# Expert blocks of a fused attention and mixture-of-experts kernel: first layer transposed, its weight fetched per block, GpSimd's gathers and scatters unrolled

## The chip, the cores and the metric

The kernel runs on one core of one Trainium2 chip. The metric is device time in microseconds, the median of several executions. "PE" is the matmul engine (its weight loads are listed as PEld), "DVE" the vector engine, "ACT" the scalar engine, "POOL" GpSimd, "SP" the sync engine, which here only issues DMAs.

## The reference, cut to what matters

A block of spatial attention, one of Nystrom attention, and then a mixture of experts, all in fp32, over T = 4096 tokens of D = 256 features. The change touches only the experts (E = 16, hidden size H = 512, two experts per token):

```python
def _L1_ffn_ref(x, W_gate, W1, W2):
    K = 2
    ...
    xf = x.reshape(-1, D)
    probs = jax.nn.softmax(xf @ W_gate, axis=-1)
    top_g, top_i = jax.lax.top_k(probs, K)
    gates = jnp.zeros((T, E), dtype=x.dtype).at[jnp.arange(T)[:, None], top_i].set(top_g)

    def step(y, params):
        W1e, W2e, ge = params
        h = jax.nn.gelu(xf @ W1e, approximate=False)
        return (y + ge[:, None] * (h @ W2e), None)
    y0 = jnp.zeros((T, D), dtype=x.dtype)
    y, _ = jax.lax.scan(step, y0, (W1, W2, gates.T))
    return y.reshape(B, L, D)
```

The output is the token rows before the experts plus y.

## The kernel before, in words

Each engine has a program of its own, written out by hand; semaphores alone order them against each other. Four samples pass through the two attention parts first (some 727 us). Each sample's rows go to the output in DRAM, and normalised to `rows_scratch` in DRAM. Then the tokens are sorted: DVE works out for each of 79 blocks of 128 slots (`BLOCKS` = 2T/128 + E - 1) which token stands in each slot (`token_of`), which row of the output it is added to (`row_of`; an empty slot has a number out of range, which the scatter skips), and which expert the block belongs to (`expert_of`). All slots of a block have the same expert. Meanwhile SP brings all weights of all experts into SBUF, 512 KB of `w1` and 512 KB of `w2` per expert, two experts at a time (lines 488 to 498), and the gates into `rows_scratch`.

The expert stage then runs over the 79 blocks, four to a pass of a loop (`ROUNDS` = 19 passes and three blocks behind them). For block n:

- POOL copies the block's column of `token_of` into `gather_ix` (L396), waits for that copy, and gathers 128 rows of 258 floats (256 features and two gates) from DRAM into one of four buffers `xg` (L399). This is done three blocks ahead: `add_rows` of block n first issues the gather of block n + 3.
- PE turns the rows by two transposes into a PSUM bank (`turn_rows`, through the helper line L506), DVE picks the gate (L1426, L1428) and copies the turned rows into `xgT` (L1429).
- PE multiplies them with the expert's `w1` (`hidden`, L885): the turned rows are the stationary operand, 512 columns of `w1` the moving one, for two halves of the contraction. An fp32 matmul takes two passes on PE, so this is 4 weight loads and 4 matmuls in the trace. The result has tokens on the partitions.
- ACT applies gelu into `hb` (L1046), PE transposes it by four (L506 again), DVE copies that to `hT` (L1436).
- PE multiplies `hT` with the expert's `w2` (L910, 8 matmuls of 256 columns in the trace). DVE multiplies with the gate into one of four buffers `y_sb` (L1444).
- POOL copies the block's column of `row_of` into `scatter_ix` (L406), waits for it, for `y_sb`, and for the scatter of the block before to have landed, and issues a scatter that adds the rows to the output in DRAM (L415). Two scatters may add to the same row, so they go one after the other.

PE's order in a block n is: transposes of gelu's result of n, `hidden` of n + 1, `turn_rows` of n + 2, second layer of n. The expert's number is read from SBUF into a register on PE (L889) twice per block, once for each layer. PE, ACT, DVE and POOL all run loops with register counters, except that POOL and DVE have the first four blocks written out.

```python
if u >= 1:
    pool.wait_ge(y_stored[u - 1], (i + 1) * 16)
elif again:
    pool.wait_ge(y_stored[3], i * 16)
```

These are the lines that hold a scatter back until the one before has landed; `y_stored[u]` counts 16 for each landed scatter out of buffer u.

## Time and profile before

| what | value |
|---|---|
| runs, device time | 1201.26, 1198.99, 1202.12 us |
| median | 1201.26 us |
| profiled execution: span from its first to its last instruction | 1197.8 us |
| profiled execution: time of its own | not given by the page; the runs above lie 1.2 to 4.3 us over its span |
| PE busy in the span | 1022.2 us, 85% |
| DVE, ACT, POOL busy | 690.5, 373.5, 361.4 us |
| DMA | 50.84 MB, mean 42 GB/s |

The span is the hardware profiler's record of one execution; busy time adds up an engine's instructions without its register, branch, semaphore and DMA-issuing ones (but POOL's indirect DMAs are in it). The expert stage begins with the routing at 727 us and its blocks fill the time from about 776 us to the end.

### The profile page before, as it was taken

The numbers are of one execution on the slowest core, as the hardware profiler recorded it, in microseconds if no ns is written. First come the engines' busy times: TensorE is split into PE (matmuls) and PEld (weight loads), VectorE is DVE, ScalarE is ACT, GpSimd is POOL, SyncE is SP. The second block draws the span as 40 slices with busy tenths as digits, with TensorE's granted clock in tenths as the row PEclk, the third lists the DMA queues.
The fourth block names the chain that finished last, engine by engine and source line by source line (L and its number), as shares of the span: only waits on it lengthen the run. The fifth ranks groups of instructions, "written<-read, shape, count | busy, mean of one in ns | idle before, by whom it ended". The sixth has DMA issues, their size and how long they took to land.

```text
span 1197.8 us, 20466 instructions
## 1 busy us (share of the span) xinstructions
PE 1022.2 (85%) x6163; PEld 654.5 (55%) x6164; DVE 690.5 (58%) x1665; ACT 373.5 (31%) x947; POOL 361.4 (30%) x514
## 2 busy tenths in 40 slices
PE   4999997999996999998999992378888888888886
PEld 2656654557663557664567660245555555545554
DVE  5767676766575767576776579923333333333332
ACT  3523463532464423455333551301111111111110
POOL 2220011310011400011500020545655556655654
PEclk8899998999997999997999996589999999999999
DMA  4000003000003000002000008933333333223220
GB/s 122 2 1 1 1 2 108 1 1 1 1 1 107 1 1 1 1 1 73 1 1 1 1 2 231 359 79 49 50 52 50 49 50 51 46 42 52 48 42 14
DMA packets 41262, 50.84 MB, mean 42 GB/s; under 512 B 10624, under 2 KB 32512, under 8 KB 41184
## 3 DMA queue, kind: packets, MB, share of 16 engines
q0 software_dynamic: 17344, 27.24, 11.9%
q1 hardware_dynamic: 23840, 22.56, 6.2%
q8 instruction: 48, 0.79, 0.3%
q14 instruction: 30, 0.25, 0.1%
HBM read 32.96 MB, written 18.78 MB: 43 GB/s over the span
## 4 chain that ended last, share of the span: by engine, by line
PE 53%; issue 15%; DVE 14%; DMA 8%; POOL 5%; ACT 3%; POOLq 1%; DVEq 0%; ACTq 0%
PE PS L506 10%; PE PS L574 10%; DMA low<-rows_scratch,gather_ix 7%; PE PS L758 6%; PE PS L535 6%; PE PS L910 5%; POOL out_dram L415 4%; PE PS L885 3%; PE PS L666 2%; PE PS L647 2%; DVE neg_max L1093 2%; PE PS L652 1%; PE PS L626 1%; PE PS L721 1%; DVE low L1444 1%
## 5 line engine op out<-in xcount | busy, mean ns | idle before, releaser
L361 POOL TENSOR_SCALAR aggr<-aggr 128x1 f32<-128x1 f32 x64 | 14.6, 228 | 592.7 <-DVE aggr L1155 592.7
L910 PE MATMUL PS<-arena,low 128*128 x632 | 156.8, 391 | 31.9 <-issue 30.9
L415 POOL DMA_INDIRECT out_dram<-low,scatter_ix x79 | 127.6, 1615 | 110.2 <-DVE low L1444 48.3
L506 PE MATMUL PS<-ident,arena 128*128 128x128 f32 x1024 | 144.6, 287 | 15.7 <-ACT arena L978 9.1
L1046 ACT ACTIVATE low<-PS 128x512 f32<-128x512 f32 x78 | 46.6, 597 | 350.3 <-PE PS L885 350.3
L885 PE MATMUL PS<-arena,low 128*128 x316 | 150.6, 599 | 0.4 <-issue 0.4
L506 PEld LDWEIGHTS PS<-ident,arena 128*128 128x128 f32 x1024 | 121.9, 150 | 47.8 <-issue 37.4
L910 PEld LDWEIGHTS PS<-arena,low 128*128 128x128 f32 x632 | 113.6, 189 | 61.9 <-issue 49.7
L1093 DVE TENSOR_REDUCE neg_max<-PS 128x1 f32<-128x1024 f32 (+1 forms) x97 | 118.4, 1221 | 48.6 <-PE PS L574 46.5
L574 PE MATMUL PS<-arena 128*128 128x512 f32 x256 | 126.7, 597 | 0.0
L964 ACT ACTIVATE arena<-PS,neg_max 128x1024 f32<-128x1024 f32 x64 | 71.3, 1114 | 132.4 <-DVE neg_max L1093 132.4
L969 ACT ACTIVATE arena<-PS,neg_max 128x128 f32<-128x128 f32 x256 | 89.8, 376 | 60.0 <-DVE neg_max L1093 60.0
L1444 DVE TENSOR_SCALAR low<-PS,slot_gate 128x256 f32<-128x256 f32 x79 | 38.2, 484 | 119.4 <-PE PS L910 85.4
L506 PEld LDWEIGHTS PS<-ident,low 128*128 128x128 f32 x474 | 56.7, 141 | 90.3 <-DMA low<-rows_scratch,gather_ix 77.1
L506 PE MATMUL PS<-ident,low 128*128 128x128 f32 x474 | 81.5, 281 | 24.5 <-DMA low<-rows_scratch,gather_ix 23.5
L399 POOL DMA_INDIRECT low<-rows_scratch,gather_ix x79 | 80.1, 1013 | 67.7 <-POOL gather_ix L396 63.9
L1426 DVE TENSOR_TENSOR gate_parts<-low,pick_of 128x2 f32<-128x2 f32 x79 | 12.7, 161 | 138.1 <-PE PS L506 136.1
L978 ACT COPY arena<-PS 128x1024 f32<-128x1024 f32 x64 | 64.5, 1008 | 61.0 <-PE PS L506 61.0
L535 PE MATMUL PS<-arena,low 128*128 128x512 f32 (+1 forms) x168 | 78.1, 609 | 5.1 <-DVE arena L1081 4.2
L758 PE MATMUL PS<-arena 128*128 128x256 f32 x320 | 80.9, 386 | 0.0
L885 PEld LDWEIGHTS PS<-arena,low 128*128 128x128 f32 x316 | 54.4, 192 | 39.1 <-issue 39.1
L758 PEld LDWEIGHTS PS<-arena 128*128 128x128 f32 x320 | 59.1, 190 | 28.3 <-issue 22.1
(195 smaller groups left out, 1488.8 us busy)
## 6 DMA issues: line engine op xcount, KB each, us to landing
arena<-in_L_ffn_W_dram SPq DMA_DIRECT2D x32, 512.0 KB, 5.2
arena<-in_x_dram SPq DMA_DIRECT2D x4, 1024.0 KB, 8.3
rows_scratch<-arena POOLq DMA_DIRECT2D x4, 1024.0 KB, 6.4
out_dram<-t POOLq DMA_DIRECT2D x4, 1024.0 KB, 9.1
low<-rows_scratch,gather_ix POOLq DMA_INDIRECT x79, 2.8
out_dram<-low,scatter_ix POOLq DMA_INDIRECT x79
arena<-in_L_attn_w_qkv_dram SPq DMA_DIRECT2D x1, 768.0 KB, 5.0
arena<-in_L_attn_w_out_dram SPq DMA_DIRECT2D x1, 256.0 KB, 5.5
```

What stands on the lines that cost most here:

```text
L399: pool.indirect_dma_start(xg[:, b, :], None, rows_dram, bass.IndirectOffsetOnAxis(ap=gather_ix[:, b:b + 1], axis=0)).then_inc(xg_loaded[b] ...
L415: pool.indirect_dma_start(out_rows, bass.IndirectOffsetOnAxis(ap=scatter_ix[:, u:u + 1], axis=0), y_sb[:, u, :], None, bounds_check=T - 1, ...
L506: mm = pe.transpose(PS[0:s.shape[1], dst_bank, n * P:n * P + s.shape[0]], s, ident[0:s.shape[0], 0:s.shape[0]])
L535: mm = pe.matmul(PS[0:m, bank, :], w[c], src[:, c, half * 512:half * 512 + 512], start=c == 0, stop=c == KC - 1)
L574: mm = pe.matmul(PS[:, b + k, :], ops[0], ops[1], start=True, stop=True)
L758: mm = pe.matmul(bank[:, o:o + 2 * M], RX[:, g, h, 0, :], RX[:, g, h].rearrange("p r m -> p (r m)"), start=True, stop=True)
L885: mm = pe.matmul(PS[:, 2 + p, :], xgT[:, p, c, :], w1_sb[:, bass.ds(e * (KC * H) + c * H, H)], start=c == 0, stop=c == KC - 1)
L910: mm = pe.matmul(PS[:, 6 + p, 0:D], hT[:, p, c, :], w2_sb[:, bass.ds(e * (HC * D) + c * D, D)], start=c == 0, stop=c == HC - 1)
L964: act.activation(Pm[:, u % 2, :], src, ACT.Exp, bias=neg_max[:, u % 2, 0:1], accum_out=row_sum[:, u % NT:u % NT + 1]).then_inc(s_exp, 1)
L969: ins = act.activation(Pm[:, u % 2, o:o + M], src[:, o:o + M], ACT.Exp, bias=neg_max[:, u % 2, h:h + 1], accum_out=head_sum[:, u % 2, h:h ...
L978: act.copy(PT[:, u % 2, :], PS[:, 2:4, :].rearrange("p b n -> p (b n)")).then_inc(t_act, 1)
L1093: dve.tensor_reduce(dst, src, AX.X, ALU.max, negate=True).then_inc(s_max, 1)
```

## The change

What it does:

- The first layer is made transposed. `w1` becomes the stationary operand (eight 128 x 128 pieces, 16 weight loads and 16 matmuls in the trace) and the turned rows `xgT` the moving one (128 columns), so that the hidden units stand on the partitions. Gelu writes `hT` directly. PE's four transposes of gelu's result, DVE's copy of them and `hb` go.
- `w1` is no longer held for all experts. SP brings the block's expert's 512 KB from HBM into one of four buffers `w1_now`, with an address from a register that it loads from `expert_of`; a fetch waits until the first layer of the block four before is done (`h_mm`). The 79 fetches are 41 MB where 8 MB were loaded before. `w2` stays resident and is loaded alone ahead.
- POOL's program is written out for all 79 blocks. Gather and scatter take their index column straight from `token_of` and `row_of`; the two copies, and the waits for them, go.
- PE reads the expert's number once a block instead of twice. DVE picks the gate beside the copy of the turned rows, in another order. ACT now also waits until the second layer of two blocks before has read `hT`. The first four blocks are written out on PE and ACT too.

The diff, cut to its core:

```diff
-        w1_sb = arena[:, 0:E * KC * H]
+        W1_BUFS = 4
+        w1_now = arena[:, 0:W1_BUFS * KC * H].rearrange("p (b n) -> p b n", b=W1_BUFS)
         w2_sb = arena[:, E * KC * H:E * (KC * H + HC * D)]
...
+            def gather(n):
+
+                pool.indirect_dma_start(xg[:, n % 4, :], None, rows_dram,
+                                        bass.IndirectOffsetOnAxis(ap=token_of[:, n:n + 1], axis=0)).then_inc(xg_loaded[n % 4], 16)
+
+            def add_rows(n):
+                if n + 3 < BLOCKS:
+                    pool.wait_ge(xt_mm, n + 1)
+                    gather(n + 3)
+                pool.wait_ge(y_copied, n + 3)
+
+                if n >= 1:
+                    pool.wait_ge(y_stored[(n - 1) % 4], ((n - 1) // 4 + 1) * 16)
+                pool.indirect_dma_start(out_rows, bass.IndirectOffsetOnAxis(ap=row_of[:, n:n + 1], axis=0),
+                                        y_sb[:, n % 4, :], None, bounds_check=T - 1, oob_is_err=False,
+                                        compute_op=ALU.add).then_inc(y_stored[n % 4], 16)
...
-                loaded = expert_dma[e % len(expert_dma)]
-                sp.dma_start(w1_sb.rearrange("p (e c h) -> p e c h", e=E, c=KC)[:, e],
-                             w1.rearrange("e (c p) h -> p e c h", p=P)[:, e]).then_inc(loaded, 16)
                 sp.dma_start(w2_sb.rearrange("p (e c d) -> p e c d", e=E, c=HC)[:, e],
-                             w2.rearrange("e (c p) d -> p e c d", p=P)[:, e]).then_inc(loaded, 16)
+                             w2.rearrange("e (c p) d -> p e c d", p=P)[:, e]).then_inc(expert_dma[e % len(expert_dma)], 16)
...
+            sp.wait_ge(tables_ready, 1)
+
+            def fetch_w1(n, u, again):
+
+                e = sp.value_load(expert_of[0:1, bass.ds(n, 1)], min_val=0, max_val=E - 1)
+                if again:
+                    sp.wait_ge(h_mm, n - 3)
+                sp.dma_start(w1_now[:, u, :].rearrange("p (c h) -> p c h", c=KC),
+                             w1.rearrange("e (c p) h -> e p c h", p=P)[bass.ds(e, 1)].rearrange("o p c h -> p (o c) h")).then_inc(w1_landed[u], 16)
...
-                for c in range(KC):
-                    mm = pe.matmul(PS[:, 2 + p, :], xgT[:, p, c, :], w1_sb[:, bass.ds(e * (KC * H) + c * H, H)],
-                                   start=c == 0, stop=c == KC - 1)
-                mm.then_inc(h_mm, 1)
...
+                pe.wait_ge(w1_landed[u], 16 * (r + 1))
+                if again:
+                    pe.wait_ge(gelu_done, n - 1)
+                for hc in range(HC):
+                    for c in range(KC):
+                        mm = pe.matmul(PS[:, 2 + p, hc * P:(hc + 1) * P], w1_now[:, u, c * H + hc * P:c * H + (hc + 1) * P],
+                                       xgT[:, p, c, :], start=c == 0, stop=c == KC - 1)
+                mm.then_inc(h_mm, 1)
...
-                transposes(pe, 4 + p, [hb[:, p, c * P:(c + 1) * P] for c in range(HC)]).then_inc(ht_mm, 1)
...
+                if ahead(i, u, 1):
+                    hidden(n + 1, i + (u + 1) // 4, (u + 1) % 4, again or u >= 1)
+                if ahead(i, u, 2):
+                    turn_rows((u + 2) % 4, i + (u + 2) // 4, p)
+                rows_out(n, p, expert(n))
...
+                act.wait_ge(h_mm, n + 1)
+                if again or u >= 2:
+                    act.wait_ge(y_mm, n - 1)
+                apart(act, "act")
+                act.activation(hT[:, p].rearrange("p c n -> p (c n)"), PS[:, 2 + p, :], ACT.Gelu).then_inc(gelu_done, 1)
...
-                dve.wait_ge(ht_mm, n + 2)
-                dve.tensor_copy(hT[:, p].rearrange("p c n -> p (c n)"), PS[:, 4 + p, :]).then_inc(hT_ready, 1)
```

How the change moves instructions on POOL, which issues every gather and scatter, in the first blocks of the expert stage: gather and scatter of one block before (a name in brackets is a semaphore that the instruction waits for; `gix` and `six` are those of the two copies),

```order
L396 COPY gather_ix<-token_of 128x1 [waits xt_mm]
L399 DMA low<-rows_scratch,gather_ix 128x258 [waits gix]
L406 COPY scatter_ix<-row_of 128x1
L415 DMA out_dram<-low,scatter_ix 4096x256 [waits y_stored0,six,y_copied]
L396 COPY gather_ix<-token_of 128x1 [waits xt_mm]
```

and in the changed kernel, where L392 is the gather and L403 the scatter:

```order
L392 DMA low<-rows_scratch,token_of 128x258 [waits xt_mm]
L403 DMA out_dram<-low,row_of 4096x256 [waits y_stored0,y_copied]
L392 DMA low<-rows_scratch,token_of 128x258 [waits xt_mm]
L403 DMA out_dram<-low,row_of 4096x256 [waits y_stored1,y_copied]
L392 DMA low<-rows_scratch,token_of 128x258 [waits xt_mm]
```

Two instructions are left of four, and the wait for the scatter before (`y_stored`) stands where it stood.

On PE, a block in the loop before (L506 are transposes, L889 reads the expert's number, L885 and L910 are the first and second layer):

```order
L506 MATMUL PS<-ident,low 128x128 [waits gelu_done]
L506 MATMUL PS<-ident,low 128x128 x3
L881 REGISTER_ALU
L883 REGISTER_ALU [waits xgT_ready]
L885 ISA [waits experts_loaded]
L885 MATMUL PS<-arena,low 128x512
L885 ISA
L885 MATMUL PS<-arena,low 128x512
L877 ISA
L506 MATMUL PS<-ident,low 128x128 [waits xg_loaded2]
L506 MATMUL PS<-ident,low 128x128
L889 ISA
```

and in the changed kernel (L889 is now the first layer, L504 the transposes, L873 reads the number, L899 is the second layer):

```order
L889 MATMUL PS<-low,arena 128x128 [waits gelu_done,w1_landed3,xgT_ready]
L889 MATMUL PS<-low,arena 128x128 x7
L504 MATMUL PS<-ident,low 128x128 [waits xg_loaded0]
L504 MATMUL PS<-ident,low 128x128
L873 TENSOR_LOAD expert_of
L873 ISA x2
L897 REGISTER_ALU [waits y_copied,gelu_done]
L899 ISA [waits experts_loaded]
L899 MATMUL PS<-arena,low 128x256
```

The four transposes ahead of the first layer are gone, and the wait for gelu has moved from them to the second layer, behind the first layer of the next block.

## Rows read from the trace of the kernel before

**Rows 1.** Page, part 1: busy us (share of the span) xinstructions of each engine.

```profile
PE 1022.2 (85%) x6163; PEld 654.5 (55%) x6164; DVE 690.5 (58%) x1665; ACT 373.5 (31%) x947; POOL 361.4 (30%) x514
```

**Rows 2.** Timeline, POOL: first and last scatter (start us, us, engine line op).

```profile
795.49 1.64 POOL L415 DMA_INDIRECT out_dram<-low,scatter_ix  x1 [10.14 <-DVE low L1444]
...
1192.64 1.57 POOL L415 DMA_INDIRECT out_dram<-low,scatter_ix  x1 [1.91 <-DMA out_dram<-low,scatter_ix]
```

**Rows 3.** Timeline of two blocks in the middle; in brackets idle before, and its releaser.

```profile
1003.25 1.61 POOL L415 DMA_INDIRECT out_dram<-low,scatter_ix  x1 [1.00 <-issue]
...
1005.89 1.01 POOL L399 DMA_INDIRECT low<-rows_scratch,gather_ix  x1 [0.82 <-POOL gather_ix L396]
...
1006.59 0.60 PE L506 MATMUL PS<-ident,low 128*128 128x128 f32 x4
...
1006.90 0.20 POOL L406 COPY scatter_ix<-row_of 128x1 int32 x1
...
1007.02 1.88 PE L885 MATMUL PS<-arena,low 128*128 x4
...
1008.75 0.44 PE L506 MATMUL PS<-ident,low 128*128 128x128 f32 x2
...
1009.60 1.99 PE L910 MATMUL PS<-arena,low 128*128 x8 [0.42 <-issue]
...
1011.63 0.48 DVE L1444 TENSOR_SCALAR low<-PS,slot_gate 128x256 f32<-128x256 f32 x1 [1.49 <-PE PS L910]
...
1013.02 1.61 POOL L415 DMA_INDIRECT out_dram<-low,scatter_ix  x1 [0.99 <-DVE low L1444]
```

**Rows 4.** Timeline, PE: second layers of blocks 0 and 1.

```profile
792.10 1.89 PE L910 MATMUL PS<-arena,low 128*128 x8
...
796.20 1.89 PE L910 MATMUL PS<-arena,low 128*128 x8
```

**Rows 5.** Windows: PE, PEld, DVE, ACT, POOL busy (x), PEclk, DMA share, GB/s.

```profile
795.00:1180.00 385.00, 336.84 (x1352) 210.27 (x1351) 139.67 (x376) 44.78 (x75) 227.39 (x300) 1.00 0.30 48
```

**Rows 6.** Chain of waits on POOL, a full scatter to the next: start us, us, what.

```profile
1126.99 3.87 DMA out_dram<-low,scatter_ix
...
1131.08 0.56 issue
...
1131.85 1.62 POOL out_dram L415
```

**Rows 7.** The same near the end, an empty scatter.

```profile
1188.96 2.74 DMA out_dram<-low,scatter_ix
```

**Rows 8.** Timeline, PE and its weight loads, sample 0's landmarks.

```profile
73.41 0.19 PEld L712 LDWEIGHTS PS<-low 128*128 128x128 f32 x1 [0.24 <-issue]
...
73.84 1.95 PE L712 MATMUL PS<-low 128*128 128x128 f32 x16
75.62 1.25 PE L721 MATMUL PS<-low,arena 128*128 128x256 f32 x5
```

**Rows 9.** DMA issues (KB each, median us to landing) and SP's timeline.

```profile
arena<-in_L_ffn_W_dram SPq DMA_DIRECT2D x32, 512.0 KB, 5.2
...
727.31 0.38 SPq L491 DMA_DIRECT2D arena<-in_L_ffn_W_dram  x1
```

**Rows 10.** Windows, columns as in rows 5.

```profile
1005.40:1006.80 1.40, 1.40 (x9) 1.20 (x8) 0.01 (x1) 0.00 (x0) 0.91 (x1) 1.00 0.78 94
728.30:728.80 0.50, 0.00 (x0) 0.00 (x0) 0.50 (x9) 0.00 (x0) 0.00 (x0) 0.50 1.59 160
754.00:780.00 26.00, 9.04 (x57) 6.71 (x57) 22.32 (x29) 7.37 (x13) 14.17 (x11) 0.50 1.04 363
```

**Rows 11.** Timeline and chain of waits at the start of the expert stage.

```profile
776.78 1.11 POOL L399 DMA_INDIRECT low<-rows_scratch,gather_ix  x1 [0.95 <-POOL gather_ix L396]
...
778.92 5.16 DMA low<-rows_scratch,gather_ix
...
785.20 3.78 PE L885 MATMUL PS<-arena,low 128*128 x4 [0.39 <-issue]
```

More of the change, by code:

```diff
@@ L92, in conv_attn_nystrom_moe_kernel @@
         lower = sb("lower", [P, P])
-        low = sb("low", [P, 5632])
+        low = sb("low", [P, 5696])
         wT_qkv = low[:, 0:1536].rearrange("p (c n) -> p c n", c=KC)
@@ L279, in conv_attn_nystrom_moe_kernel @@
         gelu_done = sem("gelu_done")
-        ht_mm = sem("ht_mm")
-        hT_ready = sem("hT_ready")
+        w1_landed = [sem(f"w1_landed{u}") for u in range(4)]
         y_mm = sem("y_mm")
         y_copied = sem("y_copied")
-        gate_chain = Chain(sem("gate_chain"), 8)
+        parts_made = sem("parts_made")
+        gate_picked = sem("gate_picked")
         gates_made = sem("gates_made")
@@ L322, in s_banks @@
             return 4 if NT <= u < 2 * NT else (4, 6)[u % 2]
-        passed = {e: sem(f"passed_{e}") for e in ("pool", "pe", "dve", "sp")}
+        passed = {e: sem(f"passed_{e}") for e in ("pool", "pe", "dve", "sp", "act")}
         def apart(eng, name):
@@ L437, in _ @@
             for n in range(3):
-                gather(n, n)
+                gather(n)
             pool.wait_ge(tables_ready, 1)
-            for u in range(4):
-                add_rows(0, u, False)
-            with pool.Fori(1, ROUNDS) as i:
-                for u in range(4):
-                    add_rows(i, u, True)
-            for u in range(len(LAST)):
-                add_rows(ROUNDS, u, True)
+            for n in range(BLOCKS):
+                add_rows(n)
         @block.sync
@@ L498, in _ @@
                 weights_in(e)
+            sp.wait_ge(tables_ready, 1)
[5 more added lines that the diff above has]
+                             w1.rearrange("e (c p) h -> e p c h", p=P)[bass.ds(e, 1)].rearrange("o p c h -> p (o c) h")).then_inc(w1_landed[u], 16)
+            for u in range(4):
+                fetch_w1(u, u, False)
+            with sp.Fori(1, ROUNDS) as i:
+                for u in range(4):
+                    fetch_w1(i * 4 + u, u, True)
+            for u in range(len(LAST)):
+                fetch_w1(4 * ROUNDS + u, u, True)
             for u in range(4):
@@ L873, in _, with turn_rows, hidden @@
             pe.wait_ge(tables_ready, 1)
-            def turn_rows(b, r, p, m):
+            expert = lambda n: pe.value_load(expert_of[0:1, bass.ds(n, 1)], min_val=0, max_val=E - 1)
+            def turn_rows(b, r, p):
                 pe.wait_ge(xg_loaded[b], 16 * (r + 1))
                 transposes(pe, p, [xg[:, b, c * P:(c + 1) * P] for c in range(KC)]).then_inc(xt_mm, 1)
-            def hidden(n, p, e):
+            def hidden(n, r, u, again):
+                p = u % 2
                 pe.wait_ge(xgT_ready, n + 1)
-                pe.wait_ge(experts_loaded, e + 1)
-                for c in range(KC):
-                    mm = pe.matmul(PS[:, 2 + p, :], xgT[:, p, c, :], w1_sb[:, bass.ds(e * (KC * H) + c * H, H)],
-                                   start=c == 0, stop=c == KC - 1)
-                mm.then_inc(h_mm, 1)
@@ L912, in expert_block @@
                 mm.then_inc(y_mm, 1)
-            with pe.Fori(0, ROUNDS) as i:
+            def expert_block(i, u, again=True):
+                p = u % 2
+                n = i * 4 + u
+                if ahead(i, u, 1):
[3 more added lines that the diff above has]
+                rows_out(n, p, expert(n))
+            turn_rows(0, 0, 0)
+            turn_rows(1, 0, 1)
+            hidden(0, 0, 0, False)
+            for u in range(4):
+                expert_block(0, u, False)
+            with pe.Fori(1, ROUNDS) as i:
                 for u in range(4):
@@ L1037, in _, with gelu @@
                     scale_rows(2 * i + b, b, True)
-            act.wait_ge(h_mm, 1)
-            act.activation(hb[:, 0, :], PS[:, 2, :], ACT.Gelu).then_inc(gelu_done, 1)
-            def next_gelu(i, u):
-                if ahead(i, u, 1):
-                    n = i * 4 + u
-                    act.wait_ge(h_mm, n + 2)
-                    act.wait_ge(ht_mm, n + 1)
-                    act.activation(hb[:, 1 - u % 2, :], PS[:, 3 - u % 2, :], ACT.Gelu).then_inc(gelu_done, 1)
-            with act.Fori(0, ROUNDS) as i:
+            act.wait_ge(tables_ready, 1)
+            def gelu(i, u, again=True):
+                p = u % 2
+                n = i * 4 + u
+                act.wait_ge(h_mm, n + 1)
[3 more added lines that the diff above has]
+                act.activation(hT[:, p].rearrange("p c n -> p (c n)"), PS[:, 2 + p, :], ACT.Gelu).then_inc(gelu_done, 1)
+            for u in range(4):
+                gelu(0, u, False)
+            with act.Fori(1, ROUNDS) as i:
                 for u in range(4):
-                    next_gelu(i, u)
+                    gelu(i, u)
             for u in range(len(LAST)):
-                next_gelu(ROUNDS, u)
+                gelu(ROUNDS, u)
         @block.vector
```

80 lines of the change are left out of this document (19 added, 61 removed).

## The prediction

> **What bounds the kernel now.** The profile's lines of busy time say PE, 85% [rows 1]; the edit sits in the last third of the span, so I read that stage alone. The issues of the scatter-add (L415) on POOL mark its 79 blocks: the first starts at 795.49, the last at 1192.64, that is 397.15 us over 78 intervals, 5.09 us each [rows 2]. In the timeline of block 41 to 42 [rows 3] the reader is to see that no engine is full, and that three rings of waits have nearly one length.
>
> *PE alone.* Where nothing was late a block took PE 796.20 - 792.10 = 4.10 us [rows 4]. PE is not the bound, though 88% "busy" (336.84 of 385 us) [rows 5].
>
> *POOL alone.* Scatter 1.62, then 1.02 to the start of the gather (a copy of 0.20 and 0.82 of waiting for it), gather 1.01, copy 0.20, some 1.00 (the idle time ahead of a scatter) to the next scatter: 4.85 [rows 3].
>
> *A ring through two blocks.* Scatter at 1003.25, gather issued at 1005.89, row transposes on PE at 1008.75 (2.86 later, when its rows had landed), L910 at 1009.60, L1444 at 1011.63 to 1012.11, the next scatter but one at 1013.02: 9.77 for two blocks, 4.88 each [rows 3].
>
> *Scatter after scatter.* Each waits for the one before to have landed. A full one landed 3.87 us after its start, and the next began 0.99 after that: 4.86 [rows 6]. An empty one (the last few blocks) took 2.74 [rows 7].
>
> So the stage is held by three rings at 4.85 to 4.88; jitter of gathers and a loop end every fourth block make 5.09 of it.
>
> **The change part by part.**
>
> *POOL's copies and semaphores go.* Per block two copies and the two waits behind them: 1.02 before the gather and the 0.20 before the scatter's wait. The gather needs nothing that is new, so I expect POOL's sequencer to prepare it while the scatter still runs (as the copy now starts without a gap behind the gather [rows 3]) and take 0 to 0.82 for its start, chosen 0.05. POOL's own ring: 1.62 + 0.05 + 1.01 + about 0.85 = 3.5. The two-block ring: 9.77 - 0.97 = 8.8, or 4.4 a block. A pass of a loop on POOL goes too.
>
> *Scatter after scatter stays.* 3.87 remains. Of the 0.99 behind it the rows show 0.22 of short sequencer steps between the landing (1130.86) and the last wait before the scatter's start (1131.08), 0.56 of issue, and 0.21 more to 1131.85 [rows 6]; without POOL's own copy, semaphore and loop register I take 0.85 of it. That is 4.72 for a full block. Blocks with few rows land sooner (2.74 at the end), and the other rings then hold at 4.4; jitter no longer adds in full, since they have 0.3 of slack. I take 4.75 a block for the first 76 intervals and leave the last two (the last is 3.68 now, from 1188.96 to 1192.64 [rows 2, 7]) at 3.7: 76 x 4.75 + 2 x 3.7 = 368.4. **Gain 397.15 - 368.4 = 28.7 us.**
>
> *First layer transposed (PE).* The four transposes of the hidden tile go: 0.43 (1006.59 to 1007.02 [rows 3]); DVE's 0.69 copy L1436 goes. L885 was 4 passes of 512 columns, 1.72; it becomes 16 passes of 128 columns, each with new weights. The same shape is in the trace: L712 issues 16 such pairs from 73.84, and L721 can start at 75.62, so 1.78 for 16, 0.11 each [rows 8]. PE's own ring: 4.10 - 0.43 + 0.06 = 3.73. Gelu now writes the operand of the second layer directly and has a whole L910 (1.7) to hide its 0.60 in. Where a gather is late, the load of the expert's number (0.85 from the transposes to L910 [rows 3]) shows again: 1.78 + 0.85 + 1.72 = 4.35, still under 4.72. I cost all this at nothing: its cover is the scatter chain. Were that chain gone, PE at 3.7 to 4.4 would be next. Bounds for the 16 passes: 1.72 below; above, 16 times a whole weight load of 0.19 [rows 8] = 3.04, if the loads did not overlap.
>
> *The weight fetch per block.* SP reads the expert's number, waits until the block four before has used the buffer, and starts 512 KB. It needs its data some 3 blocks (14 us) later; the expert loads landed in 5.2 at a full queue [rows 9]. SP has nothing else there but waits for the scatters at the end. What it costs is the DMA engines' time: with loads running they moved 363 GB/s at a share of 1.04 [rows 10], so a fetch takes 0.524 MB / 363 = 1.44 us of all 16, in a stage now at a share of 0.30 [rows 5]. Where in the block? The packets of the scatter of 1003.25 move in the slice from 1005.40 to 1006.80 (share 0.78), 2.15 to 3.55 after its start [rows 3, 10]; the gather's follow. With the rings above, and S the start of a scatter: the gather issued at S + 1.67 lands at S + 4.50, PE does transposes and L910 until about S + 7.1, then the next first layer until S + 8.9; SP issues the fetch then, and its packets start 1.0 later (727.31 issued, moving in the slice from 728.30 [rows 9, 10]): S + 10.0 to S + 11.4. With a period of 4.72 that is 0.6 to 2.0 after a scatter's start: in the gap before its packets. So I take a cost of 0.03 a block, the step from 4.72 to 4.75. Bounds: 0 (all in the gap) and 1.44 (every scatter waits for a whole fetch); no gain from it. The near row for contention is the second gather, which under the loads landed after 5.16 instead of 2.86 [rows 3, 11]: 2.3 more, but with several loads queued.
>
> *The start of the stage.* 8 MB of expert weights instead of 16 are loaded ahead; at 363 GB/s this saves about 23 us of a transfer that now runs until some 783, so the first gathers meet almost no load. The first gather starts some 0.4 before its 776.78 [rows 11], without its copy, and lands after 2.9: the first transposes come at about 779.3. The first weight fetch (the tables are ready about when that gather starts; number read, 1.0 to the first packet, 1.44) is in at about 780.5, and the first layer of block 0 starts there instead of at 785.20 [rows 11]; in the old order gelu, transposes and copy stood between the two layers, in the new one the first layer of block 1 does. PE runs at a granted clock of 0.50 (1.2 GHz) over the routing [rows 10] and L885 took 3.78 there instead of 1.88 [rows 3, 11]; the new passes pay the same doubling, some 3.6. Scatter 0 then comes at 789 instead of 795.49. **Gain 6 us** (bounds 2 and 8).
>
> *The end* stays: 5.1 us after the last scatter's start.
>
> **Sum.** 28.7 + 6 = 34.7 against the profiled execution: span 1197.8 becomes 1163.1. The page gives a span and no time of that execution; the median of the runs, 1201.26, lies 3.5 above the span, and I keep that: **1166.5 us**.
>
> **The rule weighed.** The Trainium skill ("DMA: Bandwidth & Descriptors", Queues, rings and completion order) says that a DMA engine drains a whole packet of some 9 to 17 descriptors from one ring before it turns to another. No row of before shows the two queues mixed at this rate. By it a scatter that meets a fetch would wait for nearly the whole of the fetch's part on each engine instead of sharing, and the result would be rival D's in place of C's.
>
> **The rivals.**
>
> A. *The gather's start is not prepared ahead* (0.82 stays between scatter and gather). For it: every gather now starts 0.82 behind its copy. Against: that wait includes a result. The two-block ring is then 9.6, 4.8 a block, and with jitter as now (0.2) 5.0: 76 x 5.0 + 7.4 = 387.4, gain 9.8 + 6: 1185.
>
> B. *The fetch meets the scatter or the gather in part*, some 0.3 a block on the ring: 76 x 5.05 + 7.4 = 391.2, gain 6 + 6: 1189. For it: the gap of 0.6 to 2.0 is a sum of many steps and ends just before the packets at 2.1.
>
> C. *Slower: every scatter waits for the fetch.* Place: the packets of L415. Price by rows: its packets take 1.4 in all [rows 10]; shared with a fetch of 1.44, about half of that is added. It decides from (397.15 + 6 - 7.4) / 76 = 5.21 a block on, that is from 0.46 over my 4.75. At 0.72: 76 x 5.47 + 7.4 = 423, loss 26 - 6: 1221. Against: the phase worked out above, which locks the fetch to the scatter's gap, and a share of DMA of only some 0.6.
>
> D. *Slower still: each scatter waits for a whole fetch*, 1.44: 76 x 6.19 + 7.4 = 478, loss 81 - 6: 1276. Against: as for C; and the gather's 2.3 under load had several fetches ahead of it.
>
> E. *Weight loads don't overlap*: first layer 3.04, PE's ring 3.04 + 0.85 + 1.72 = 5.6: 78 x 5.6 = 437, loss 40 - 6: 1235. Against: rows 8 show the same pairs at 0.11.
>
> F. *The change doesn't do what it says*: the scatter chain was the only bound and keeps its 4.86 and the jitter: 1195, gain from the start alone.
>
> **How the numbers follow.** Forecast 0.58, A 0.10, B 0.12, C 0.09, D 0.02, E 0.01, F 0.08. The forecast's own range is 1150 (copies' removal brings 4.6 a block, 12 less, and a start of 8) to 1180. The range reaches over A, B and F and leaves out C, D and E: 1150 to 1202. About 0.3% (3.6 us) is what a measurement of this kernel can tell from no change; faster by more: forecast, A, most of B and half of F, 0.80; within: 0.07; slower: 0.13.
>
> **What would show it.** Scatter issues 4.7 apart, with the landing of the scatter before as what ended POOL's wait; gathers starting as the scatter's issue ends; no copies on POOL; 16 weight loads at 0.11 spacing, about 1.8 from first to last; PE and ACT waiting on nothing of SP's; DMA share up to 0.6; first scatter near 789. Wrong it would be if scatters land later than 3.9 after their start (C), if gathers land after more than 2.9 and PE waits for them (B), or if a gap stands ahead of each gather (A).

## The result, and the profile after

| | before | after |
|---|---|---|
| median of the runs | 1200.12 us (4 runs) | 1210.95 us (4 runs, 1206.63 to 1210.98) |
| profiled span | 1197.8 us | 1209.3 us |
| first scatter to 77th (76 intervals) | 5.13 us each | 5.34 us each |
| first scatter starts | 795.49 | 791.15 |

The ratio of the times is 1.0079 (95% interval 1.006 to 1.0099). By it the change is 9.5 us slower, where 34.7 us faster was forecast, and 1210.95 lies outside the range of 1150 to 1202. The page of after, parts 1, 5 and 6, beside [rows 1, 9]:

```profile
PE 996.6 (82%) x6794; PEld 718.1 (59%) x6795; DVE 628.7 (52%) x1586; ACT 373.8 (31%) x947; POOL 327.1 (27%) x356
...
L403 POOL DMA_INDIRECT out_dram<-low,row_of x79 | 126.2, 1598 | 201.5 <-DMA out_dram<-low,row_of 158.8
...
L392 POOL DMA_INDIRECT low<-rows_scratch,token_of x79 | 78.7, 996 | 28.8 <-issue 23.5
...
arena<-in_L_ffn_W_dram SPq DMA_DIRECT2D x95, 512.0 KB, 4.4
...
low<-rows_scratch,token_of POOLq DMA_INDIRECT x79, 3.3
out_dram<-low,row_of POOLq DMA_INDIRECT x79, 4.5
```

PE, DVE and POOL are busy for less time and a smaller share than before, and the program is longer. The line of L403 (the scatter-add, once L415) says where it sits: POOL stands idle for 201.5 us ahead of 79 scatters, 158.8 of them until the scatter before has landed. Of the 76 scatters behind the first, 64 have this landing as their last wait. A gather lands after 3.3 us (2.8 on the page of before), a scatter after 4.5.

The chain of waits of after on three scatters in a row, beside [rows 6] (start us, us, what):

```profile
999.29 4.27 DMA out_dram<-low,row_of
1003.57 0.02 issue
1003.59 0.02 POOLq L402
1003.61 0.04 issue
1003.65 0.03 POOLq L403
1003.68 0.77 issue
1004.45 4.45 DMA out_dram<-low,row_of
...
1009.01 0.77 issue
1009.78 4.50 DMA out_dram<-low,row_of
```

From a landing to the next scatter's start it is now 0.88 (0.02 + 0.02 + 0.04 + 0.03 + 0.77) instead of 0.99. But the landing itself is 4.27 to 4.50 instead of 3.87. So the gain of 0.1 and the loss of 0.4 to 0.6 stand side by side.

The timeline of after over the block that starts at 1004.45, beside [rows 3]:

```profile
1004.23 0.60 ACT L1051 ACTIVATE low<-PS 128x512 f32<-128x512 f32 x1 [4.96 <-PE PS L889]
1004.25 5.55 SPq L487 DMA_DIRECT2D arena<-in_L_ffn_W_dram  x2
1004.42 0.20 PEld L504 LDWEIGHTS PS<-ident,low 128*128 128x128 f32 x2 [0.53 <-DMA low<-rows_scratch,token_of]
1004.42 0.44 PE L504 MATMUL PS<-ident,low 128*128 128x128 f32 x2 [0.34 <-DMA low<-rows_scratch,token_of]
1004.45 1.60 POOL L403 DMA_INDIRECT out_dram<-low,row_of  x1 [2.25 <-DMA out_dram<-low,row_of]
...
1005.48 1.99 PE L899 MATMUL PS<-arena,low 128*128 x8 [0.62 <-ACT low L1051]
1006.35 1.00 POOL L392 DMA_INDIRECT low<-rows_scratch,token_of  x1 [0.30 <-issue]
1007.09 1.97 PEld L889 LDWEIGHTS PS<-low,arena 128*128 128x128 f32 x16
1007.31 1.95 PE L889 MATMUL PS<-low,arena 128*128 128x128 f32 x16
```

POOL has no copy left, and the gather starts 1.90 after the scatter (2.64 in [rows 3]). The 16 narrow passes of the first layer (L889) take 1.95 to the end of the last one, as those of L712 in [rows 8]. SP issues the fetch at 1004.25, 0.2 before the scatter. Three windows over the same block show what that meets (us, PE, PEld, DVE, ACT, POOL busy, clock, DMA share, GB/s), beside [rows 10]:

```profile
1004.45:1005.05 0.60, 0.41 (x2) 0.17 (x2) 0.04 (x1) 0.38 (x1) 0.60 (x1) 1.00 0.00 0
1005.05:1007.15 2.10, 1.67 (x8) 1.49 (x9) 0.52 (x3) 0.00 (x0) 1.80 (x2) 1.00 0.90 212
1007.15:1008.90 1.75, 1.75 (x17) 1.72 (x16) 0.48 (x1) 0.00 (x0) 0.20 (x1) 1.00 0.87 164
```

The middle one, 0.6 to 2.7 after the scatter's start, moves 0.445 MB (212 GB/s for 2.10 us) of the fetch's 0.524; the fetch's end, the scatter's packets and the next gather's stand in the last one.

The trace also has every single DMA packet. In it the fetch's packets run from 0.8 to 2.8 after a scatter's start, 2.1 from the first one's start to the last one's end (medians of blocks 4 to 72), and the scatter's first packet comes at 2.76, where without a fetch it comes at 2.17. In the block shown the fetch runs from 0.82 to 3.07, and the scatter's first packet starts at 3.02. The two go together block by block (correlation 0.98 between the fetch's end and the scatter's first packet): in the five blocks whose fetch was done by 2.2 the scatter's first packet came at 2.17 to 2.24, in the other 64 it came 0.07 before the fetch's end at the median. The Trainium skill ("DMA: Bandwidth & Descriptors", Queues, rings and completion order) has a DMA engine drain a whole packet, typically some 9 to 17 descriptors, from one ring before it turns to another. The trace agrees: a fetch is 256 records of 2 KB, on average 16 for each of the 16 engines. If a record is one descriptor, that is by this figure one or two packets of an engine (an estimate), and the scatter waits for what is left of the fetch and does not share with it.

The start of the stage, beside [rows 11], and its end, beside [rows 2]:

```profile
776.41 0.98 POOL L392 DMA_INDIRECT low<-rows_scratch,token_of  x1 [0.30 <-issue]
...
781.26 3.62 PE L889 MATMUL PS<-low,arena 128*128 128x128 f32 x16
...
785.71 2.02 PE L889 MATMUL PS<-low,arena 128*128 128x128 f32 x16 [0.83 <-DMA arena<-in_L_ffn_W_dram]
...
791.15 1.62 POOL L403 DMA_INDIRECT out_dram<-low,row_of  x1 [10.70 <-DVE low L1451]
```

```profile
1197.10 1.58 POOL L403 DMA_INDIRECT out_dram<-low,row_of  x1 [2.33 <-DVE low L1451]
1200.65 1.55 POOL L403 DMA_INDIRECT out_dram<-low,row_of  x1 [1.97 <-DMA out_dram<-low,row_of]
1204.16 1.55 POOL L403 DMA_INDIRECT out_dram<-low,row_of  x1 [1.96 <-DMA out_dram<-low,row_of]
```

The 76 intervals are (1197.10 - 791.15) / 76 = 5.34.

### The profile page after: what moved, and what is told of

Its sections match the earlier page's. It is cut to its first block, busy times and chain, and to the rows that moved or that the text cites. A ratio compares the mean times of both kernels' runs of the same rounds, so it can differ in the third digit from the quotient of the medians.

```text
span 1209.3 us, 21170 instructions
## 1 busy us (share of the span) xinstructions
PE 996.6 (82%) x6794; PEld 718.1 (59%) x6795; DVE 628.7 (52%) x1586; ACT 373.8 (31%) x947; POOL 327.1 (27%) x356
## 4 chain that ended last, share of the span: by engine, by line
PE 43%; DMA 25%; issue 13%; DVE 13%; ACT 3%; POOL 2%; POOLq 0%; DVEq 0%; SPq 0%; ACTq 0%
DMA out_dram<-low,row_of 21%; PE PS L572 9%; PE PS L504 8%; PE PS L756 6%; PE PS L533 5%; DMA low<-rows_scratch,token_of 3%; PE PS L664 2%; PE PS L645 2%; DVE neg_max L1100 2%; PE PS L650 1%; POOL out_dram L403 1%; PE PS L624 1%; PE PS L719 1%; DVE low L1398 1%; ACT arena L981 1%
## 5 line engine op out<-in xcount | busy, mean ns | idle before, releaser
L899 PE MATMUL PS<-arena,low 128*128 x632 | 160.9, 399 | 46.0 <-issue 27.4
L403 POOL DMA_INDIRECT out_dram<-low,row_of x79 | 126.2, 1598 | 201.5 <-DMA out_dram<-low,row_of 158.8
L899 PEld LDWEIGHTS PS<-arena,low 128*128 128x128 f32 x632 | 116.2, 194 | 75.9 <-issue 62.4
L889 PEld LDWEIGHTS PS<-low,arena 128*128 128x128 f32 x1264 | 156.1, 194 | 5.5 <-issue 1.1
L504 PE MATMUL PS<-ident,arena 128*128 128x128 f32 x1024 | 143.7, 286 | 16.2 <-ACT arena L981 9.7
L889 PE MATMUL PS<-low,arena 128*128 128x128 f32 x1264 | 156.2, 277 | 0.8 <-DMA arena<-in_L_ffn_W_dram 0.8
L504 PEld LDWEIGHTS PS<-ident,arena 128*128 128x128 f32 x1024 | 121.2, 149 | 48.1 <-issue 37.7
L392 POOL DMA_INDIRECT low<-rows_scratch,token_of x79 | 78.7, 996 | 28.8 <-issue 23.5
L756 PEld LDWEIGHTS PS<-arena 128*128 128x128 f32 x320 | 59.1, 190 | 28.3 <-issue 22.1
L504 PE MATMUL PS<-ident,low 128*128 128x128 f32 x158 | 34.5, 300 | 46.9 <-DMA low<-rows_scratch,token_of 46.7
L572 PEld LDWEIGHTS PS<-arena 128*128 128x128 f32 x256 | 43.3, 190 | 21.2 <-issue 19.9
```

The source lines that it names most:

```text
L392: pool.indirect_dma_start(xg[:, n % 4, :], None, rows_dram, bass.IndirectOffsetOnAxis(ap=token_of[:, n:n + 1], axis=0)).then_inc(xg_loaded ...
L403: pool.indirect_dma_start(out_rows, bass.IndirectOffsetOnAxis(ap=row_of[:, n:n + 1], axis=0), y_sb[:, n % 4, :], None, bounds_check=T - 1, ...
L504: mm = pe.transpose(PS[0:s.shape[1], dst_bank, n * P:n * P + s.shape[0]], s, ident[0:s.shape[0], 0:s.shape[0]])
L572: mm = pe.matmul(PS[:, b + k, :], ops[0], ops[1], start=True, stop=True)
L756: mm = pe.matmul(bank[:, o:o + 2 * M], RX[:, g, h, 0, :], RX[:, g, h].rearrange("p r m -> p (r m)"), start=True, stop=True)
L889: mm = pe.matmul(PS[:, 2 + p, hc * P:(hc + 1) * P], w1_now[:, u, c * H + hc * P:c * H + (hc + 1) * P], xgT[:, p, c, :], start=c == 0, stop ...
```

## The experiments

**Theory (T in the expectations):** the fetch's packets stand ahead of the scatter's on the DMA engines, scatters land some 0.6 later, and the chain of scatters carries that to the end. **Rivals:** that the new first layer, a wait for weights or PE's half clock costs the time (R1, R7), that POOL's copies were no bound (R2), that the fetch's traffic costs the same wherever it lies, by its bytes or through the gathers (R3, in each expectation's own words), that POOL's unrolling is worth little beside the fetch (R4), that without the scatters' chain PE alone would be next (R5) and the new first layer would pay (R6), that half-clock stretches come from late gathers alone (R8). Three groups of kernels ran, each beside runs of the kernel before.

### The parts alone

`no_fetch` is the kernel after without the fetches behind the first four blocks. It leaves out their weights: each later block multiplies with the weights of one of the first four.

```diff
-            with sp.Fori(1, ROUNDS) as i:
-                for u in range(4):
-                    fetch_w1(i * 4 + u, u, True)
-            for u in range(len(LAST)):
-                fetch_w1(4 * ROUNDS + u, u, True)
...
-                pe.wait_ge(w1_landed[u], 16 * (r + 1))
+                pe.wait_ge(w1_landed[u], 16)
```

> Leaves out the weight fetches of the blocks behind the first four: the first layer of all later blocks multiplies with whatever of the first four weights lies in its buffer, so the output is not the reference's. Theory T (a scatter's packets wait behind the fetch's on each DMA engine, and the chain scatter - landing - scatter is the bound): scatters land 3.85 after their start again instead of 4.45, are 4.7 apart, and the time is about 1210.95 - 76 x 0.62 = 1164. Rival R1 (the transposed first layer or PE's half-clock stretches cost the time): the scatters stay over 5.2 apart and the time stays over 1200.

Measured: 1173.2 us, ratio 0.9761 (0.9742 to 0.978), 37.8 us below after. Intervals 4.83, median 4.72, landing 3.8. R1 falls. The theory's 1164 was missed by 9: only 38 of 76 scatters wait last for the landing before them; 37 wait for DVE's copy of the second layer's result (L1446), the ring through two blocks.

`unroll_only` is the kernel before with POOL's unrolled gathers and scatters, and nothing else.

```diff
-                pool.tensor_copy(gather_ix[:, b:b + 1], token_of[:, bass.ds(n, 1)]).then_inc(gix, 1)
-                pool.wait_ge(gix, n + 1)
...
+                pool.indirect_dma_start(xg[:, n % 4, :], None, rows_dram,
+                                        bass.IndirectOffsetOnAxis(ap=token_of[:, n:n + 1], axis=0)).then_inc(xg_loaded[n % 4], 16)
```

> The kernel before with only POOL's part of the change: no index copies, all 79 blocks written out. Theory T: the old first layer with no fetch leaves the same scatter chain of 4.7, or PE's ring with the load of the number (0.43 + 1.72 + 0.85 + 1.83 = 4.83) if a gather is late: 4.8 a block, 1200 - 76 x 0.3 = 1177. Rival R2 (POOL's copies were not a bound, the two-block ring or the jitter was): within 5 us of 1200.

Measured: 1171.77 us, ratio 0.9762 (0.9745 to 0.9778). Intervals 4.74, first scatter at 794.90. Its chain of waits on POOL, a window over one scatter of it, and POOL's groups from 800 to 1150:

```profile
973.19 3.66 DMA out_dram<-low,row_of
976.85 0.02 issue
976.87 0.02 POOLq L406
976.89 0.04 issue
976.93 0.03 POOLq L407
976.96 0.76 issue
977.72 3.86 DMA out_dram<-low,row_of
```

```profile
968.52:970.60 2.08, 1.66 (x8) 1.07 (x7) 0.74 (x3) 0.60 (x1) 1.77 (x2) 1.00 0.00 0
970.60:972.30 1.70, 1.70 (x10) 1.34 (x9) 0.63 (x2) 0.00 (x0) 0.81 (x1) 1.00 0.84 106
```

```profile
L407 POOL DMA_INDIRECT out_dram<-low,row_of x74 | 118.3, 1598 | 136.1 <-DMA out_dram<-low,row_of 93.7 <-DVE low L1431 39.2 <-issue 3.2
L396 POOL DMA_INDIRECT low<-rows_scratch,token_of x74 | 73.4, 992 | 22.5 <-issue 22.2 <-PE PS L493 0.3
```

For the first 2.08 us after the scatter's start the DMA engines move nothing at all, and landings are at 3.7 to 3.9. This is the forecast's chain, 3.87 + 0.85, and it stands: 28.7 us below the kernel before (1200.5 in this group) in one small edit. R2 falls, and the expectation's 1177 was 5 too high. Both kernels without fetches do alike (1173.2 and 1171.77), so the transposed layer is worth nothing here: `no_fetch` starts its scatters 3.0 us earlier and has intervals longer by 0.09.

`fetch_on_old` puts the traffic alone onto `unroll_only`: 512 KB a block into two spare buffers that nothing reads, issued where the change issues it, behind `h_mm` (and, as there are only two buffers, behind the landing of the load two before).

```diff
+            for n in range(4, BLOCKS):
+                sp.wait_ge(h_mm, n - 3)
...
+                sp.dma_start(spare[:, n % 2, :].rearrange("p (c h) -> p c h", c=KC),
+                             w1.rearrange("e (c p) h -> p e c h", p=P)[:, n % E]).then_inc(w1_landed[n % 2], 16)
```

> unroll_only with the fetch's traffic alone added: SP brings 512 KB of first-layer weights per block into spare buffers that nobody reads, at the same event as in the changed kernel (the end of the first layer of four blocks before); first layer and resident weights as before. Theory T (the traffic and its place is what costs, not the transposed layer): the scatters land after 4.3 to 4.5, 5.2 to 5.35 a block, 1172 + 76 x 0.55 = 1213. Rival R7 (the transposed layer or PE's waiting for its weights has a large part in it): under 1190.

Measured: 1213.03 us, ratio 1.0097 (1.008 to 1.0114). Intervals 5.31. The chain of waits and POOL's groups from 800 to 1150:

```profile
1003.37 4.39 DMA out_dram<-low,row_of
...
1007.88 0.76 issue
1008.64 4.69 DMA out_dram<-low,row_of
```

```profile
L409 POOL DMA_INDIRECT out_dram<-low,row_of x66 | 105.5, 1599 | 159.8 <-DMA out_dram<-low,row_of 157.6 <-DVE low L1442 2.3
```

Traffic that no computing engine waits for costs 41 us (1213.03 - 1171.77; 40 by the two ratios), with the old first layer and all weights resident. The same 0.76 of launch is there, the same POOL work; 66 scatters fit into the 350 us instead of 74, as in after. This settles the cause: neither the layer nor a wait for weights is needed for it, and its trace has no stretch of half clock in the blocks. The expectation's 1213 was met; R7 falls.

`old_pool` is after with POOL's old copies, semaphores and loop.

```diff
-            for n in range(BLOCKS):
-                add_rows(n)
+            for u in range(4):
+                add_rows(0, u, False)
+            with pool.Fori(1, ROUNDS) as i:
+                for u in range(4):
+                    add_rows(i, u, True)
```

> The changed kernel with POOL's part of before (index copies, semaphores, loop). Theory T: the fetch holds the scatters as in the changed kernel, and the longer path from landing to issue (0.99 instead of 0.85) and the longer POOL ring come on top: 5.4 to 5.6 a block, 1215 to 1230. Rival R4 (once the fetch holds the scatters, POOL's own work no longer matters): within 4 us of 1211.

Measured: 1232.31 us, ratio 1.0287 (1.0245 to 1.0329), intervals 5.57. Beside the fetch the unrolling is still worth 21 us; the intervals lie in the expected 5.4 to 5.6, the time 2 above the expected 1215 to 1230, and R4 falls.

### The fetch's size and place

`half_fetch` brings only the first half of each later weight; the other half of the contraction uses stale weights.

```diff
-                sp.dma_start(w1_now[:, u, :].rearrange("p (c h) -> p c h", c=KC),
+                cs = 1 if again else KC
+                sp.dma_start(w1_now[:, u, :].rearrange("p (c h) -> p c h", c=KC)[:, 0:cs],
```

> Fetches only the first of the two halves of the weight (256 KB) behind the first four blocks, so the output is not the reference's. Theory T: the fetch ends some 0.7 us earlier, at about 1.9 after a scatter's start, before the scatter's packets: nearly the whole gain of leaving it out, 1165 to 1175. Rival R3 (cost by bytes): half of what no_fetch gains, about 1188.

Measured: 1182.49 us, ratio 0.9848 (0.9831 to 0.9864), intervals 4.97, median 4.84. That is between the theory's 1165 to 1175 and R3's 1188: a quarter of the 38 us remains at half the bytes. The loop is shorter, so `h_mm` and the fetch come later against the scatter, at 1.3 to 2.5, and the scatter's first packet at 2.32. The cost is not in proportion to the bytes; it fits the part of a fetch that reaches past 2.17, for which the theory had placed the end too early (1.9).

`fetch_at_y` issues the fetch when DVE has copied an earlier block's result, just ahead of the scatter.

```diff
-                    sp.wait_ge(h_mm, n - 3)
+                    sp.wait_ge(y_copied, n - 1)
```

> The changed kernel with one wait exchanged: SP starts a block's fetch when the second layer's result has been copied (y_copied, a block later than the buffer is free) and not at the end of the first layer (h_mm), so that the fetch's packets move at another point of the block: about 0.6 before to 1.2 after a scatter's start instead of 0.6 to 2.7 after it. Theory T: scatter packets start at 2.2 after the issue again, landing after 3.9 to 4.0, 4.8 a block, about 1170. Rival R3 (any fetch traffic costs the same wherever it lies, by the DMA engines' share or by HBM): unchanged, about 1211.

Measured: 1189.97 us, ratio 0.9913 (0.9896 to 0.9929). The fetch runs at 0.2 to 2.4 (medians), the scatter's first packet at 2.23, landings at 3.9. All bytes move, and half of the cost is gone: R3's 1211 falls, and the theory's 1170 was missed by 20. The six executions took 1183.46 to 1191.5 us, and the trace is of the shortest.

`fetch_at_ymm` issues it behind the second layer.

```diff
-                    sp.wait_ge(h_mm, n - 3)
+                    sp.wait_ge(y_mm, n - 3)
```

> As fetch_at_y, but SP waits for the end of the second layer (y_mm) and not for its copy, 0.6 us earlier. The fetch's packets then should run from about 0.4 before a scatter's start to 1.7 after it and be done before the scatter's packets at 2.2. Theory T: landing after 3.85 in nearly all blocks, 4.8 to 4.85 a block, 1175 to 1180. Rival R3: the gather's packets (3.6 to 4.3 after the scatter's start) are met instead and PE waits for them: about 1190 or more.

Measured: 1198.62 us, ratio 0.9987 (0.9957 to 1.0016). The ten executions scatter, from 1191.76 to 1209.91; the trace is of one that took 1194.98. The theory was right on the scatters and missed the time (1175 to 1180): first packet at 2.17, landing 3.8, median interval 4.74, but a mean of 5.11. R3's number (1190 or more) was met. The slowest tenth of the gathers land after 4.4 or more (3.8 in `no_fetch`). The timeline and two windows around one of the long intervals:

```profile
1012.11 1.60 POOL L403 DMA_INDIRECT out_dram<-low,row_of  x1 [1.96 <-DVE low L1451]
...
1013.54 0.44 PE L504 MATMUL PS<-ident,low 128*128 128x128 f32 x2 [1.20 <-DMA low<-rows_scratch,token_of]
...
1014.60 3.58 PE L899 MATMUL PS<-arena,low 128*128 x8 [0.62 <-issue]
...
1019.61 1.60 POOL L403 DMA_INDIRECT out_dram<-low,row_of  x1 [4.60 <-DVE low L1451]
```

```profile
1014.80:1018.20 3.40, 3.40 (x10) 2.65 (x9) 0.00 (x0) 0.00 (x0) 0.21 (x1) 0.50 0.33 67
1018.20:1060.00 41.80, 33.66 (x223) 29.99 (x223) 8.86 (x33) 4.78 (x8) 20.73 (x16) 1.00 0.64 146
```

A gather was late, PE idled 1.20 and 0.62, and then PE's granted clock stood at 0.50 (1.2 GHz) for 3.4 us: L899 took 3.58 instead of 1.99, and the interval 7.5. There are six such stretches in its blocks, three in after's.

`ymm_warm` is `fetch_at_ymm` with four transposes of the identity more per block, ahead of the first layer; nothing reads them.

```diff
+                transposes(pe, 4 + p, [ident[:]] * HC)
```

> fetch_at_ymm with four more transposes of the identity on PE in each block, into banks that nobody reads, at the place where the old kernel turned gelu's result. In fetch_at_ymm PE's granted clock fell to 0.5 for six stretches of 3.4 or more in the blocks, each beside an interval of 6 to 7.6 between scatters, against none in the kernel before. If PE's idle time in the block brings the clock down, the work that the change took away kept it up: 0 to 2 stretches, about 1180. Rival R8 (the stretches come from late gathers alone): as many as in fetch_at_ymm, 1195 to 1200.

Measured: 1182.02 us, ratio 0.9832 (0.9815 to 0.9848), one stretch instead of six; R8 falls. More work on PE made the kernel 17 us faster (10.5 between the two profiled spans, 1193.3 and 1182.8). This version fetches and is 19.6 us below the kernel before (1201.58 in its group), as `fetch_at_y` already was by 10.5.

### Without the chain of scatters

In these, odd blocks scatter into a scratch tensor, and each scatter waits for the last but one. They leave the odd blocks' sum out of the output. `two_transposed` is `no_fetch` with that split (and with its stale weights), `two_old_layer` is `unroll_only` with it, `two_all` the kernel after with it.

```diff
-                if n >= 1:
-                    pool.wait_ge(y_stored[(n - 1) % 4], ((n - 1) // 4 + 1) * 16)
-                pool.indirect_dma_start(out_rows, bass.IndirectOffsetOnAxis(ap=row_of[:, n:n + 1], axis=0),
+                if n >= 2:
+                    pool.wait_ge(y_stored[(n - 2) % 4], ((n - 2) // 4 + 1) * 16)
+                pool.indirect_dma_start(other_rows if n % 2 else out_rows, bass.IndirectOffsetOnAxis(ap=row_of[:, n:n + 1], axis=0),
```

> no_fetch with every second block's scatter going to a scratch tensor instead of the output, so that a scatter waits for the one two blocks before and not for the last (half of the rows are missing in the output, and the weights are those of no_fetch). Shows which ring comes next when the scatter chain is gone. From the trace of no_fetch: scatter 1.60, gather at 1.90, landed 2.86 later, transposes to second layer 1.06, to the copy's end 2.57, to the scatter 0.83: 9.2 for two blocks, 4.6 a block, 1173 - 76 x 0.23 = 1156. Rival R5 (PE at 3.7 a block is next): 1173 - 76 x 1.1 = 1090.

Measured: 1166.94 us, ratio 0.9718 (0.9699 to 0.9737). Intervals alternate between 3.7 and 5.7, mean 4.79. The theory's 4.6 (1156 us) was not reached, and R5, PE's own 3.7 as the next bound, falls altogether: only every other interval is so short. Of 76 scatters 67 wait last for DVE's copy of the second layer's result (L1447), none for a landing.

> unroll_only with the same split of the scatters: every second block's rows go to a scratch tensor, half of the output is missing. The old first layer, whose PE ring with the number's load is 4.83 when a gather is late and 4.10 when not. Theory: 4.5 to 4.8 a block, 1152 to 1172, so that the transposed first layer is worth nothing or little even without the chain. Rival R6 (the transposed layer pays 0.4 a block once the chain is gone): this one stays at 1172 while two_transposed falls by 30.

Measured: 1161.1 us, ratio 0.9674 (0.9655 to 0.9693), mean 4.62. With the chain gone only 0.12 a block is won: the ring through two blocks, forecast at 4.4, is right behind it. The old first layer is again no slower than the transposed one; here it is faster, by 5.8 us. R6 falls.

> The changed kernel, fetches and all, with every second block's scatter going to a scratch tensor, so that a scatter waits for the one two blocks before (half of the rows are missing in the output). Theory T: the fetch costs time only because each scatter waits for the last; with that gone the fetch's 0.6 on a landing is hidden, and it runs as two_transposed plus what the gathers lose: 1167 to 1180. Rival R3 (the traffic slows everything, gathers as much): over 1195.

Measured: 1189.25 us, ratio 0.9914 (0.9888 to 0.9941), mean 5.05, between theory (up to 1180) and R3 (over 1195). Without the chain the fetch still costs 22 us (from 1166.94): gathers land after 3.4 instead of 2.9, and 71 of 76 scatters behind the first wait last for DVE's copy (L1452), the end of the two-block ring. So the theory that a fetch costs only through the chain fell short, and R3 holds part of the truth: the fetch delays the gathers too, and in after the chain of scatters, which is longer still, hides most of it.

### A version that beats both

`unroll_late` is `unroll_only` with the last two experts' loads held back until the first three gathers have landed.

```diff
+                if e == 14:
+                    for u in range(3):
+                        sp.wait_ge(xg_loaded[u], 16)
```

> unroll_only, and SP starts the loads of the last two experts only when the first three gathers have landed, which now share the DMA engines with them (5.16 instead of 2.86 for the second). Expected: first scatter 4 to 5 us earlier (795 to 790.5), the rest unchanged: 1167. If the last two experts' loads then meet the first scatters, 1169.

Measured: 1166.52 us, ratio 0.9707 (0.969 to 0.9723). The time was met, its reason only in part: the first scatter starts at 793.94, 1.0 earlier than in `unroll_only`, and the profiled span is 2.6 shorter (1165.8 against 1168.4), while the medians differ by 5.3. The two ran in different groups, and what the rest of it is stays open. It is the fastest version with the full output, 35 us below the kernel before (1201.58 in its group).

## Why the prediction was wrong, point by point

**The step that failed is the fetch's "cost of 0.03 a block"**, and in it the duration. "363 GB/s, so a fetch takes 1.44" came from a stretch in which several loads stood in the queues and kept all 16 engines supplied [rows 10]. In after a fetch of 512 KB, alone on the engines, took 2.1 (0.524 MB / 2.12 = 247 GB/s). The start of its packets was forecast at 0.6 after the scatter's start and is 0.8; its end was forecast at 2.0, just inside the gap before 2.15, and is 2.8, outside it. Rival B named this fragility ("ends just before the packets at 2.1") and priced it at 0.3.

**The other half is what happens when the two meet.** Rival C took "about half" of 1.44 for sharing, 0.72. The runs show neither sharing nor D's whole fetch: the scatter's packets wait for what is left of the fetch, 2.76 - 2.17 = 0.59 at the median. That is the rule that the prediction weighed, but not the price that it drew from it (D): the fetch was two thirds through when a scatter came up. That makes the interval 0.51 longer than `no_fetch`'s, 5.34 against 4.83, 76 x 0.51 = 39 us, and the two kernels' times differ by 38. C's place and sign are what happened (a landing later than 3.9), and 5.34 lies above the 5.21 from which it decides; that its price was near, 0.72 for 0.59, is luck, as it was worked out from sharing. It had a chance of 0.09. B's sign showed as well, gathers landing after 3.3. The argument against C, "the phase worked out above, which locks the fetch to the scatter's gap", rested on a margin of 0.15 (2.0 against 2.15) at the end of a sum of many steps. And nothing locked it: `h_mm` moves with PE, PE with the gathers, and the fetch starts anywhere from 0.2 to 1.5 (10th and 90th percentile). An estimate from after's 69 blocks tells the two faults apart: with the measured starts and the forecast's 1.44 a fetch would reach past 2.17 by 0.23 on average; with the measured lengths and a start of 0.6, by 0.56; the measured mean is 0.75.

**The rest of the sum, term by term.**

- *POOL's copies* ("28.7 us"): right in `unroll_only`, and its parts too: landing 3.7 to 3.9, then 0.87. That it is right to the tenth is partly luck: the forecast's 4.75 a block held 0.03 for a fetch that `unroll_only` lacks, and of its 76 scatters only 52 have the landing as their last wait, 23 the ring through two blocks; it has 4.74.
- *The gather's start* ("chosen 0.05"): wrong. POOL idles 0.30 between scatter and gather (rival A had 0.82). The two-block ring, forecast at 4.4 a block, is 4.6 by the steps of `no_fetch`'s trace and 4.79 when it stands alone (`two_transposed`). In after it holds 10 of 76 scatters, in `no_fetch` 37, so it was not as far behind the chain as forecast.
- *The 16 passes* ("1.78"): right: 1.78 in after from the first pass at 789.52 to the next transposes at 791.30, at full clock. Rival E falls.
- *The start* ("gain 6"): 4.3. The first layer of block 0 starts at 781.26 (forecast about 780.5), but block 1's waits for its own weights until 785.71, for which the forecast had no term. `no_fetch` starts its first scatter at 791.88 and `unroll_only` at 794.90, so of the 4.3 the unrolling is 0.6 and the new loads and layer order 3.0; the last 0.7 is not told apart.
- *PE's clock*: the forecast has no term for half clock within the blocks. There are three stretches at 0.50 in after's blocks, none in before's.
- *F* (the chain keeps 4.86) falls with `unroll_only`.

**The sum as it came out:** -28.7 from before to `unroll_only`, +1.4 from there to `no_fetch` (3.0 earlier at the start, given back by intervals of 4.83 for 4.74, one stretch of half clock among them), +37.8 from there to after: +10.5. The medians of before and after differ by 10.8, and the ratio says 9.5. How much of the 37.8 is two more stretches of half clock is not told apart; `fetch_on_old` has none and pays 41.

Not tried: a transposed first layer with all its weights resident and no fetch. `no_fetch` stands in for it only in time.

## What to carry to other kernels

A transfer that "fits into a gap" needs its own duration when it is alone in the queue, not the rate of a full one, and a margin larger than the jitter of what triggers it. Where a chain of small DMAs sets the end, a bulk transfer on the same engines can be paid in that chain's latency, here at a mean DMA share of 0.60 and though nobody waits for the transfer; tie its trigger to the chain itself (`fetch_at_y` won back half), or keep the data resident. Split a change into its parts before accepting or rejecting it: here one part was worth 29 us and another cost 38.

## What the runs showed of the hardware

**A scatter does not share with a fetch.** In after its packets start as the last of the fetch's ends (2.76 against 2.83 at the median), though they come over different queues. At the median none of the fetch's 256 packets is still to start when the scatter's first one starts; in nine blocks of ten it is at most 12.

**PE's clock can fall after short idle times in a stage that seems busy.** A stretch at half clock (1.2 GHz) from after's timeline:

```profile
924.14 0.44 PE L504 MATMUL PS<-ident,low 128*128 128x128 f32 x2 [1.63 <-DMA low<-rows_scratch,token_of]
...
925.20 3.68 PE L899 MATMUL PS<-arena,low 128*128 x8 [0.63 <-issue]
```

PE had idled 1.63 and 0.63; L899 then took 3.68 instead of 1.99, and the interval from 923.68 to 930.29 was 6.6. Every kernel with the transposed layer has one to six such stretches of 3.4 us in its blocks, and no kernel with the old layer has one. In after PE is busy 79% of the time (276.38 of 350 us, from 800 to 1150); `unroll_only` is at 92% (322.16 of 350). Before each stretch PE had idled 0.9 to 2.4 us and then 0.4 to 1.0. Idle times of 1.2 us or more are 10 in after's 76 intervals, 17 in `fetch_at_ymm`'s and none in `ymm_warm`'s, the one run that only gave PE more to do. But neither the share nor one long idle time alone decides it: after has 10 such idle times and 3 stretches, `fetch_on_old` at 85% (299.23, with the old layer) has no stretch, and `ymm_warm`, at 90% (314.84), still has one. What does decide it stays open.
